# Batch 1's gate-and-up input split by token and turned by transposing DMA transfers instead of by TensorE

## The reference, cut to what matters

```python
x = _layernorm(x + attn(x, Wqkv, bqkv, Wo, bo))
x = _layernorm(x + _wkv(w, u, k=x, v=ctx))
Wg = (gate_w - 128) * gate_scale[:, None]     # Wu and Wd alike
g = einsum('bsh,ih->bsi', x, Wg)              # 2048 gate columns
u = einsum('bsh,ih->bsi', x, Wu)
x = _layernorm(x + einsum('bsi,hi->bsh', silu(g) * u, Wd))
```

## Time and profile before

| what | value |
|---|---|
| median of three executions | 708.41 us |
| the profiled execution: span from first to last instruction | 709.9 us |
| TensorE busy | 671.4 us, 95% |
| VectorE, ScalarE, GpSimd busy | 72%, 70%, 56% |
| DMA, mean over the span | 77 GB/s |
| share of TensorE in the chain that ended last | 61% |
| mean granted TensorE clock | 0.989 |

### The profile page before, as it was taken

One profiled execution on the slowest core, in us unless ns is written; L12 is line 12 of the kernel. 1 busy time (PEld: TensorE's weight loads), 2 busy tenths in 40 slices (PEclk: granted clock), 3 DMA queues, 4 the chain that ended last, 5 costly groups with the idle time before them and its releaser, 6 DMA issues.

```text
span 709.9 us, 12525 instructions
## 1 busy us (share of the span) xinstructions
PE 671.4 (95%) x4290; PEld 380.8 (54%) x4290; DVE 513.2 (72%) x1220; ACT 496.1 (70%) x1143; POOL 395.7 (56%) x508
## 2 busy tenths in 40 slices
PE   8979999899988989799989999999999999999996
PEld 3435555445445545454445454544456797578845
DVE  4676767787888899989755569858777786655644
ACT  5798889789897879978787873384754855336620
POOL 6035735846999664864596654885771634103321
PEclk9999999999999999989999999999999999999999
DMA  7878944322332136460071002000001000000001
GB/s 239 249 218 235 217 145 135 98 75 79 124 102 78 38 85 163 120 143 16 8 120 60 1 0 75 16 31 0 1 1 44 17 1 2 30 31 1 1 16 45
DMA packets 45024, 54.33 MB, mean 77 GB/s; under 512 B 5921, under 2 KB 33825, under 8 KB 44961
## 3 DMA queue, kind: packets, MB, share of 16 engines
q1 hardware_dynamic: 41264, 46.85, 21.6%
q0 software_dynamic: 3264, 6.29, 5.4%
q10 hardware_dynamic: 432, 0.39, 0.2%
HBM read 45.00 MB, written 12.71 MB: 81 GB/s over the span
## 4 chain that ended last, share of the span: by engine, by line
PE 61%; DVE 13%; ACT 10%; POOL 5%; issue 5%; DMA 4%; SPq 1%; POOLq 0%; DVEq 0%; ACTq 0%
PE psb L1160 12%; PE psb L1133 8%; PE psb L996 6%; PE psb L1184 5%; PE psb L1182 5%; PE psb L1104 4%; PE psb L1072 4%; PE psb L1027 4%; DVE ee L1530 3%; PE psb L1039 3%; PE psb L1056 3%; DVE x L1607 2%; PE psb L1120 2%; PE psb L1083 2%; ACT L1330 1%
## 5 line engine op out<-in xcount | busy, mean ns | idle before, releaser
L1530 DVE CUSTOM_DVE_ANT_0 ee<-psb,mask,clip 128x512 f32<-128x512 f32 (+3 forms) x256 | 131.3, 542 | 24.9 <-PE psb L1039 22.3
L1278 ACT ACTIVATE ee<-ee,nm 128x512 f32<-128x512 f32 (+3 forms) x256 | 142.2, 560 | 1.4 <-DVE nm L1530 1.4
L1938 POOL TENSOR_TENSOR hl<-ring,hh 128x512 f16<-128x512 f32 x64 | 80.1, 1264 | 86.7 <-ACT hh L1414 57.3
L1288 ACT ACTIVATE ee<-psb 128x256 f32<-128x256 f32 (+1 forms) x192 | 94.6, 523 | 31.0 <-PE psb L1056 21.0
L1182 PE MATMUL psb<-wd,hh 128*128 128x512 f16 x240 | 91.0, 379 | 0.0
L1184 PE MATMUL psb<-wd,hl 128*128 128x512 f16 x240 | 91.0, 379 | 0.0
L1868 POOL TENSOR_SCALAR_AFFINE_SELECT ee<-ee 128x256 f32<-128x256 f32 x128 | 56.8, 452 | 60.7 <-ACT ee L1288 59.9
L1039 PE MATMUL psb<-ks,qs 128*128 128x512 f16 (+3 forms) x256 | 72.5, 305 | 8.3 <-DVE nm L1530 6.1
L1056 PE MATMUL psb<-qs,ks 128*128 128x128 f16 (+3 forms) x256 | 60.1, 306 | 9.6 <-ACT ee L1288 7.5
L996 PE MATMUL psb<-xh,wqk 128*128 128x512 f16 x240 | 61.8, 385 | 1.7 <-POOL xh L1830 1.2
L1885 POOL TENSOR_TENSOR rs<-ve,half 128x1 f32<-128x1 f32 (+1 forms) x24 | 20.5, 854 | 72.0 <-DVE ve L1599 71.7
(11 more groups left out here) (217 smaller groups left out, 1668.2 us busy)
## 6 DMA issues: line engine op xcount, KB each, us to landing
qs<-parts SPq DMA_DIRECT2D x48, 128.0 KB, 2.7
ks<-parts SPq DMA_DIRECT2D x45, 128.0 KB, 2.9
parts<-qhl SPq DMA_DIRECT2D x16, 256.0 KB, 2.2
parts<-khl SPq DMA_DIRECT2D x16, 256.0 KB, 2.2
x<-in_x SPq DMA_DIRECT2D x4, 1024.0 KB, 6.8
ct<-in_ctxT SPq DMA_DIRECT2D x4, 1024.0 KB, 5.1
out<-x SPq DMA_DIRECT2D x16, 256.0 KB, 2.0
xt<-in_xT SPq DMA_DIRECT2D x14, 256.0 KB, 3.4
```

The costliest lines, as they stand in the source:

```text
L1278: e.activation(dst, dst, ACT.Exp, bias=NM[:, n % 4, col:col + 1], scale=-1.0, accum_out=DEN[:, n % 4, col:col + 1]).then_inc(sem("exp"), 1)
L1288: e.activation(ET[H % ET_SLOTS][:, base:base + width], PSB[:, bank["turn", H, item], 0:width], ACT.Exp, scale=SC).then_inc(sem("et"), 1)
L1530: e.tensor_tensor_reduce(E[H % E_SLOTS][:, EOFF[i]:EOFF[i] + w], PSB[:, bank["score", H, i], 0:w], MASK[:, S - w:S], -SC, CLIP[:, i:i + 1] ...
L1938: e.tensor_tensor(HS[it][1][:], pair(b, it // 2)[:, it % 2, :] if b in SEVEN else ring(b, it)[1], HS[it][0][:], ALU.subtract).then_inc(sem ...
```

## The change

It concerns batch 1 alone. ScalarE rounds 64 times x with tokens still on the partitions (`token_high`, into `BYTOKEN[0]`, the buffer `s1b`), VectorE takes what is left (`token_low`, into `s2b`), and then ScalarE's queue issues two `dma_start_transpose` per token tile, eight in all (`turn_tokens`, the new piece `xtr`). Each moves 128 tokens x 512 float16 (128 KB) from SBUF to SBUF and turns it on the way into four blocks of 128x128. The sixteen TensorE transposes of batch 1 and their four bank uses are gone. The first gate matmul of batch 1 waits for all eight transfers (`s_xtr` at 128). The two buffers are later used for sums of weights, and the sum that reuses them waits for the transfers too. Two semaphores of the biases are merged into one.

```diff
--- before.py
+++ after.py
@@ -56,11 +56,13 @@
 SEVEN = (2, 3)
 PAIRS = IT // 2
 
-SIGNAL = {"snap1": "snap", "snap5": "snap", "snap6": "snap", "c11": "summed", "c12": "summed", "c22": "summed"}
+SIGNAL = {"snap1": "snap", "snap5": "snap", "snap6": "snap", "c11": "summed", "c12": "summed", "c22": "summed", "scale_bqk": "biases", "bo": "biases"}
 
 PART_READ = {1: 1, 2: 0, 3: 0, 4: 3, 5: 1, 6: 2, 7: 2}
 
 EARLY = 8
+TURNED = 1
+TURN_WAIT = 4
 TAIL = 20
 HS_ORDER = (0, 1, 2, 3, 8, 9, 10, 11, 4, 5, 6, 7, 12, 13, 14, 15)
 FF = 1000
@@ -372,6 +374,11 @@
 
     def x2t(b, c):
         tt.flush(("norm", 1, b, 0, T))
+        if b == TURNED:
+            for name in ("x2h", "x2l"):
+                add(name, b, c)
+            late(TURN_WAIT, lambda: add("xtr", b, c))
+            return
         tt.unit("x2t", b, c)
         add("x2t", b, c)
         if b in SEVEN:
@@ -394,7 +401,7 @@
         def part(p):
             name = "gate" if p < 2 else "up"
             if it == 0 and p == 0:
-                tt.flush(("x2l", b, T - 1))
+                tt.flush(("xtr" if b == TURNED else "x2l", b, T - 1))
             if p % 2 == 0:
                 tt.unit(name, b, it, pool=pools[p // 2])
                 tt.unfinished.add((name, b, it))
@@ -756,6 +763,7 @@
         YS = sb(f, "ys", [P, 2, D], F32)
         S1A, S1B, S2B = (sb(f, n, [P, I], F16) for n in ("s1a", "s1b", "s2b"))
     CTS = [CT, CT, CT2, CT]
+    BYTOKEN = tuple(w[:].rearrange("p (t n) -> p t n", t=T) for w in (S1B, S2B))
     RINGS = [(RING01[:, 0, :], RING01[:, 1, :]), (RING01[:, 2, :], RING01[:, 3, :]), (RING2[:, 0, :], RING2[:, 1, :])]
 
 
@@ -848,6 +856,9 @@
     def by_p(b, m, j):
         return by("p", b, m, j)
 
+    def by_turned_x2():
+        return sem("xtr"), 2 * 16 * T
+
     def by_zero(name, k):
         return sem("zero_" + name), k + 1
 
@@ -939,6 +950,8 @@
                     3: (wg[:, kk, :], wu[:, kk, :], ALU.subtract),
                     4: (wg[:, 2 + kk, :], WSUM[2][kk], ALU.subtract)}[j]
         q.wait_ge(*by("wo", B - 1, T - 1))
+        if j in (1, 2) and kk == 1:
+            q.wait_ge(*by_turned_x2())
         if j == 4:
             q.wait_ge(sem("out0"), 16 * T)
         if j in (2, 4):
@@ -1124,8 +1137,11 @@
             bk, wt, s = bank[name, b, it], wg if name == "gate" else wu, b % 2
             if half == 0:
                 emptied((name, b, it))
-                pe.wait_ge(*by("x2h", b, T - 1))
-                pe.wait_ge(*by("x2l", b, T - 1))
+                if b == TURNED:
+                    pe.wait_ge(*by_turned_x2())
+                else:
+                    pe.wait_ge(*by("x2h", b, T - 1))
+                    pe.wait_ge(*by("x2l", b, T - 1))
                 pe.wait_ge(*by_zero("wg", T - 1))
                 pe.wait_ge(*by_zero("wu", T - 1))
             for k in (2 * half, 2 * half + 1):
@@ -1346,16 +1362,26 @@
             e.activation(X[b][:, t, :], X[b][:, t, :], ACT.Identity, bias=SHIFT[:, j:j + 1],
                          scale=RS[:, 8 + b, t:t + 1]).then_inc(sem("norm2"), 1)
 
+        def turn_tokens(b, t):
+            act.wait_ge(*by("x2l", b, t))
+            for k, to in enumerate((x2h, x2l)):
+                e.dma_start_transpose(to[:, b, :, t * P:(t + 1) * P], BYTOKEN[k][:, t, :]).then_inc(sem("xtr"), 16)
+
+        def token_high(b, t):
+            act.wait_ge(*by_norm(1, b, t))
+            act.wait_ge(*by("wo", B - 1, T - 1))
+            e.activation(BYTOKEN[0][:, t, :], X[b][:, t, :], ACT.Copy, scale=WS).then_inc(sem("x2h"), 1)
+
         def x2_high(b, c):
+            if b == TURNED:
+                token_high(b, c)
+                return
             act.wait_ge(*by("x2t", b, c))
             if b >= 2:
                 act.wait_ge(*by("up", b - 2, IT - 1))
             if b == 0:
                 act.wait_ge(*by("qk", NG - 1, "k"))
                 act.wait_ge(*by("v", B - 1, T - 1))
-            elif b == 1:
-                act.wait_ge(*by_put(NG - 1, "q"))
-                act.wait_ge(*by_put(NG - 1, "k"))
             e.activation(x2h[:, b % 2, c, :], PSB[:, bank["x2t", b, c], :], ACT.Copy, scale=WS).then_inc(sem("x2h"), 1)
 
         def x_full(b, c):
@@ -1485,6 +1511,8 @@
                 ek(*a)
             elif name == "x2h":
                 x2_high(*a)
+            elif name == "xtr":
+                turn_tokens(*a)
             elif name == "th":
                 th(*a)
             elif name == "xf":
@@ -1639,7 +1667,15 @@
             dve.wait_ge(sem(f"{name}_in{k * T // dst.shape[1]}"), 16)
             e.tensor_scalar(dst[:, k, :], dst[:, k, :], -128.0, None, ALU.add).then_inc(sem("zero_" + name), 1)
 
+        def token_low(b, t):
+            dve.wait_ge(*by("x2h", b, t))
+            e.scalar_tensor_tensor(out=BYTOKEN[1][:, t, :], in0=X[b][:, t, :], scalar=WS, in1=BYTOKEN[0][:, t, :],
+                                   op0=ALU.mult, op1=ALU.subtract).then_inc(sem("x2l"), 1)
+
         def x2_low(b, c):
+            if b == TURNED:
+                token_low(b, c)
+                return
             s = b % 2
             dve.wait_ge(*by("x2h", b, c))
             e.scalar_tensor_tensor(out=x2l[:, s, c, :], in0=PSB[:, bank["x2t", b, c], :], scalar=WS, in1=x2h[:, s, c, :],
@@ -1709,7 +1745,7 @@
         def r3(b, t):
             j = b * T + t
             dve.wait_ge(*by("yd", b, t))
-            dve.wait_ge(*by("x2t", b, T - 1))
+            dve.wait_ge(*by("x2h" if b == TURNED else "x2t", b, T - 1))
             e.tensor_tensor(X[b][:, t, :], YS[:, j % 2, :], X[b][:, t, :], ALU.add).then_inc(sem("r3"), 1)
             stats(2, b, t, "r3")
 
@@ -1740,7 +1776,7 @@
                 e.bn_aggr(MV[:, 2 * B + B - 1, T - 1, :], ST4[:]).then_inc(sem("ba2"), 1)
             elif name == "scale_bqk":
                 dve.wait_ge(sem("bqk"), 16)
-                e.tensor_scalar(BQK[:], BQK[:], WS, None, ALU.mult).then_inc(sem("scale_bqk"), 1)
+                e.tensor_scalar(BQK[:], BQK[:], WS, None, ALU.mult).then_inc(sem("biases"), 1)
             elif name == "low":
                 low(*a)
             elif name == "weigh":
@@ -1758,7 +1794,7 @@
             elif name == "bo":
                 dve.wait_ge(*by("bvo"))
                 dve.wait_ge(*by_consts2())
-                e.tensor_tensor(BO[:], PSB[:, bank["bvo",], :], BO[:], ALU.add).then_inc(sem("bo"), 1)
+                e.tensor_tensor(BO[:], PSB[:, bank["bvo",], :], BO[:], ALU.add).then_inc(sem("biases"), 1)
             elif name == "split_wo":
                 dve.wait_ge(sem("woh"), 1)
                 dve.wait_ge(sem("warm"), 1)
```

## The result

The changed kernel takes 720.5 us (median; 719.0 to 721.5) against 708.7 us of the kernel before in the same comparison: a ratio of 1.0149, 95% interval [1.0119, 1.0178], slower by 8 to 13 us. (The ratio is not the quotient of the two medians, 1.0167, which lies inside the interval.) The forecast was 719.5 us in a range of 712 to 737. The profiled execution spans 716.9 us.

A forecast was written before the change was run, and what follows sets the result against it. TensorE, busy 95% of the span, was taken to bound the kernel, batch 1's data arriving just in time. Later gate +10.45, lead -1.24, restart +1.9 gave +11.1 us: 708.4 + 11.1 = 719.5 us, range 712 to 737.

The forecast's parts named there:

- the later gate: Batch 1's first gate matmul on TensorE moves from 455.35 to 465.8 us, when the eighth transfer lands: +10.45 us.
- the restart: After 12 us of idling, TensorE's first ten matmuls run at the lower 1.2 GHz clock: +1.9 us, bounds 0 and twice this.
- the lead: TensorE runs ahead of ScalarE by PSUM banks; 1.2 us lost before batch 1's ninth `it` comes back: -1.24 us.
- The removed transposes are worth nothing: 16 TensorE transposes gone save 1.74 us, but gate's input is not there, so the saving turns into waiting.
- First issue 4.0 us after the roundings begin: ScalarE's in-order queue runs roundings, next `ek` and batch 0's norm first, so the first transfer issues at 456.1 us.
- 1.0 us an issue, by `stg`: Each transposing transfer holds ScalarE's queue 1.0 us, bounds 0.35 and 2.15, taken from `stg`, the row nearest in form.
- 2.7 us from issue to landing: Each 128 KB transfer lands 2.7 us after issue, bounds 2.0 and 8.3; the eighth, issued at 463.1, lands at 465.8.
- VectorE's remainders between 2.48 us and four times 1.72: Four `x2l` with two SBUF inputs might stretch beside GpSimd, ending between 455.2 and 459.6 us; costs little.
- The seed's delay is covered: ScalarE's seed behind the eight issues moves from 460.82 to about 464.1; GpSimd and VectorE wait for later silus anyway.
- The turning itself sets the pace: Rival: each transfer starts only when the one ahead landed, eight take 21.6 us; 731.4 us in all; chance 0.24.
- Hidden by ScalarE: Rival: ScalarE's path sets the end, so only the first silu's delay counts, +3.4 us, 711.8 us; chance 0.11.
- Fast hand-off: Rival: ScalarE issues all eight in about 0.35 us, moving side by side, no restart; +1.9 us, 710.3 us; chance 0.07.

The follow-up runs named there:

- e10: Kernel before without batch 1's 16 transposes and without transfers; roundings and remainders cut to one column, batch 0's halves read; ratio 1.0012 [0.9983, 1.0041].
- e7: Changed kernel with batch 1's roundings, remainders and eight transfers one planner step earlier, still from ScalarE; timed +4.6 us [2.9, 6.2] against before.
- e9: Changed kernel with early roundings, high halves in one transfer, low in four, all from SyncE, remainders behind the first scan; ratio 1.0029 [1.0009, 1.0049] against before.
- e8: Changed kernel with eight transfers of half the width (128x256, 64 KB), chunks 0 and 1 read twice; timed +9.1 us [7.4, 10.9] against before.
- e5: Changed kernel with the same eight transfers issued by SyncE's queue, three slots earlier in the list; timed +10.0 us [7.0, 12.9] against before.
- e4: Changed kernel with 50 useless matmuls ahead of batch 1's gate to fill TensorE's idle time; 718.65 us, ratio 1.0126 against before.
- e2: Changed kernel with only the four high-half transfers, batch 0's low halves read instead; 715.1 us as ratio over the 708.4 us of before.
- e6: Changed kernel with two transfers of 512 KB instead of eight, halves laid out by chunk then token; ratio 1.0133 [1.0099, 1.0167] against before.
- e3: Changed kernel without any transfers, split by token kept, batch 1's gate and up reading batch 0's halves; ratio 1.0015 [0.9998, 1.0031] against before.

## Why the prediction was right

The forecast's mechanism was the one that happened, and the sum was 11.1 us for a measured 11.48: +10.58 for the later gate (forecast 10.45), +2.14 for the restart (1.9), -1.24 for the lead (-1.24). Inside the first of these, two terms were off, in opposite directions.

- *The removed transposes are worth nothing.* Right: TensorE came to the gate early and idled, 12.34 us for the forecast 12.2. e10 shows it without the transfers as well, within 1.2 us. The forecast read "just in time" off the roundings; x itself lay ready 9.6 us ahead of them (e7), which changes nothing in the sum but is what e9 could use.
- *First issue 4.0 us after the roundings begin (456.1 - 452.11).* Wrong, 449.45 - 447.61 = 1.84. "ScalarE's queue is in order: after the roundings come the next `ek` and the norm of batch 0, then the eight transfers" is true of the program. But an issue does not wait until the activations ahead of it have run; it waits for its own semaphore, here for the first remainder. The step was forecast 2.2 us too long.
- *1.0 us an issue, by `stg`.* Too low: 1.33 from start to start ((458.78 - 449.45)/7). Over seven steps that is 2.3 us too little. e8 and e5 showed what it is: a cost of its own, some 1.27 us, of a transposing issue, whatever its width up to 128x512 and on either queue. Plain issues of the same queue took 0.35 to 0.45.
- *2.7 us from issue to landing.* 2.51 for the last. With these three errors together the last landing came 458.78 + 2.51 - 447.61 = 13.68 us after the roundings' start, where 465.8 - 452.11 = 13.69 was forecast. That the two agree to a hundredth is luck: the first issue was forecast more than twice as late as it came and the time of an issue a quarter too short, and only the landing was sized right, within 0.2 us. Right by reason is the form of the sum.
- *The restart, 1.9 us.* The first 16 matmuls took 5.75 us against 3.61 before, +2.14, and 2.2 by e4. The rule of the Trainium skill ("TensorE: Matmul & The Clock Gate", Part 1) that an idle array falls back to 1.2 GHz is what the row of 455 to 465 us shows, with its 0.50. Unlike the forecast's row from the start of the program, the profile prints the lower clock here.
- *The lead's lost time comes back, 1.24 us.* Right: from the first gate matmul to the ninth `it` it took 30.17 us before and 31.07 now, of which 2.14 are the slow start, so 1.24 came back. e4, with neither wait nor slow start, took 28.95.
- *VectorE's remainders between 2.48 us and four times 1.72.* 3.87, and without cost, as forecast: a pair of issues takes 2.66 us and a remainder 0.97, so from the second on they are always ahead.
- *The seed's delay is covered.* It ran 12.57 us after the roundings' start (forecast 12.0). e5, which takes it away, gains nothing.

The rivals. *The turning itself sets the pace* falls: each transfer lands 2.5 us after its own issue although the next is issued after 1.33, so two overlap, and half the width changes nothing. The 1309 ns of the Trainium skill ("VectorE: DVE Perf Modes", The three transpose paths), there for one 128x128 block, is near the time of one issue here (1289 to 1321 ns), which holds four such blocks; taken as a price per block it would have given 751.7 us, an estimate from that page. *Hidden by ScalarE* falls: the first silu came 17.43 us after the roundings instead of 12.02, +5.4, while the ninth `it` came 11.5 later: 27.5 us after the silu, not 21.4, so TensorE's path is the longer one. e7, though, is this rival's own case: once the transfers come early, ScalarE's path decides. *Fast hand-off* falls with the issue time.

## What to carry to other kernels

Ask when the operand of a moved transpose is made, and not how busy the engine is that transposes. Here the roundings began 3.2 us before the gate, and an exchange of 1.7 us of TensorE's time for a row of eight issues put 12 us of waiting on the path. Ask also whether the place in the list is the data's or only the list's: the normalised x lay ready 12.9 us before the gate (455.35 - 442.50), and e9 used that. A transposing transfer costs about 1.3 us of its queue and 2.5 us to land, so few and large ones, from a queue on which nothing else waits, and only where there is room: from the first rounding to the last landing it was 13.7 us in the changed kernel, and 12.6 to the gate in e9 (450.50 - 437.85). And before hiding such a transfer, measure what its removal could give at all: a kernel that leaves the work out (e10) said at most 1.2 us.

## What the runs showed of the hardware that was not expected

- One issue of a transposing transfer between two SBUF buffers of f16 holds the queue 1.19 to 1.33 us over all kernels, with medians of 1.23 to 1.30, at 128x256 and at 128x512, on ScalarE's and on SyncE's queue alike; at 512 KB of one go 2.0 and 3.8 us. The two last are single rows of one kernel (and 2.0 again in e9), and why the second took longer isn't known; it was issued while the first was under way.
- Landing is 2.4 to 2.5 us after the issue for 64 and 128 KB, 3.3 to 3.6 for one of them in some kernels (the second of the eight in the changed one), and 4.4 to 5.3 for 512 KB.
- ScalarE's queue issued a transfer at 449.45 us while activations that stand ahead of it in the program started at 449.69 and 450.83. The reverse doesn't hold: an activation that stands behind the transfers waits for all of them to be issued (12.88 us in e7).
- VectorE's `scalar_tensor_tensor` with both inputs from SBUF (x in f32, its rounding in f16): four take 2.49 us with GpSimd idle or at pieces of one column beside them (e7), 3.87 beside its 128x512 operations (the changed kernel and e2 to e6 and e8), 4.62 in e9, with single ones from 0.67 to 1.76. With one input from PSUM four took 2.48 while GpSimd ran 128x512 operations at 452.28 and 453.45. Moving the operand from PSUM to SBUF thus made VectorE 1.4 us slower, for which nobody waited in the changed kernel, and TensorE did in e3.
- The slow start doesn't grow with the idling before it. The gate's first 16 matmuls took 5.31 us after 3.2 us (e3), 6.03 after 4.0 (e7), 5.27 after 7.1 (e2), 5.47 after 8.5 (e6) and 5.75 after 12.3 (the changed kernel), and 3.63 after 1.5 (e4).
